# Two feed-forwards to an attention in a fused macaron block: a new order of steps, with residuals kept in DRAM

## The chip, the cores and the metric

The kernel runs on one core of a Trainium2 chip. The metric is the device time of one execution in microseconds (us); lower is better. The core's engines each work through an instruction list of their own, in order, and wait for one another by semaphores: TensorE (PE in the profile), VectorE (DVE), ScalarE (ACT), GpSimd (POOL) and SyncE (SP), which here issues every DMA.

## What is computed

The input is x of 8 batches x 512 tokens x 512 features. Every batch goes through three parts:

```
x = x + 0.5 * ffn(layernorm(x))          # ffn1
x = x + attention(layernorm(x))
x = x + 0.5 * ffn(layernorm(x))          # ffn2

ffn(h):       hidden = silu(h @ W1.T) * (h @ W3.T)         # 2048 wide
              return fwht(hidden) @ W2.T                   # Hadamard transform, normalised
attention(h): q, k, v = rmsnorm(h, qkv_norm_w) @ ternary(qkv_w).T     # 16 heads of 32
              for each of 4 chunks of 128 tokens, with a state S of 32 x 32 a head:
                  o = scale * ((q k^T * decay mask) v + (q * decay) S)
                  S = decay^128 * S + (k * decay)^T v
              return rmsnorm(rmsnorm(o, norm_w), proj_norm_w) @ ternary(proj_w).T
```

All three parts of a batch depend on one another in turn; different batches don't. Both feed-forwards use the same weights.

## The kernel before

Weights are turned, split and (for W2) Hadamard-transformed once, during the first feed-forward, and stay in SBUF. An fp32 value is kept as a sum of two fp16 numbers, high and low; a product of two such values takes three matmuls (high x high, high x low, low x high), and one with the ternary weights two.

**A feed-forward** (`feed_forward`, L211) runs over 16 hidden tiles j of 128. Per tile TensorE does three main steps of 12 matmuls each of 128x512: `gate` j into g_bank, `lin` j into l_bank (L1271), and `down` j - 1 into the four d_banks (L1286). ScalarE takes the silu of g_bank (L742), VectorE multiplies it with l_bank into `hfull` (L986), ScalarE casts the high half (L755), VectorE subtracts for the low half (`low`, L993). g_bank, l_bank, `gate` and `hfull` exist once: gate j + 1 waits for silu j, lin j + 1 for hfull j. At the end VectorE adds the four d_banks to the residual (`resid`, L1001).

**Slots.** The order of all work is written out in one list of steps per place, and every engine walks the same list, doing its part of each step. Between the main steps lie 48 slots: slot 3j stands after gate j, 3j + 1 after lin j, 3j + 2 after low j (down j - 1 stands before low j). Other work is hung into slots.

**The attention** (`attention_slots`, L237) has four head groups g of 128 columns. With b the slot of a group's first scores, b, b + 1, b + 2, b + 3 hold the four `score` steps, b + 2 to b + 5 the four `pv` steps; q(g) is at b - 6 (b - 5 for the first group), k(g) one later, `klow` two later, `kturn` at b - 1; groups are 7 slots apart. q, k and score share bank a_bank0; kturn, kv and pv use a_bank1; v and proj alternate. A score is taken from its bank by VectorE (L1170). q and k are split, stored to DRAM and loaded back into `qs` and `ks` in another layout by SP (L535 to L554). After the last group come `ostat`, the norm `o`, and `proj` (four 8-matmul steps, two banks by turns), whose result VectorE adds to x1 (L1199) to give x2.

**A norm** (`norm_steps`, L227) is three slot entries. `pre`: four bn_stats and seven small operations on VectorE (L1018 to L1038, for `o` L1055 to L1070), a power on GpSimd (L595), `prep` of tile 0. `tr0` and `tr1`: for each tile of 128 tokens VectorE's `prep` into the one buffer `centred` (L1087 and L1090 for qkv, L1092 for o, L1095 else), ScalarE's cast (L764), VectorE's low half `split` (L1111), and a DMA transpose on SP (L560) into an operand buffer: xt for ffn1, zt for q, k, v, yt for o and ffn2. The next tile's prep waits for the split of the one before.

**Places** (PLAN, L419). Batch 0's ffn1 with the preparation of weights (FIRST); batch 1's ffn1 with batch 0's attention; then by turns an ffn2 without attention (SECOND, for batch i - 1, with the norm ffn1 at slots 10, 14, 15 and the norm qkv at 28, 32, 33) and batch i + 1's ffn1 with batch i's attention (WITH_ATTENTION, from slot 0); at the end batch 6's ffn2 with batch 7's attention, and batch 7's ffn2 alone. In the first attention's place and the last one the norm qkv stands at slots 0, 1, 2 and q(0) at 4. The norm ffn2 stands behind proj in the attention's own place (slots 40 to 42, or 44 to 46), and its ffn2 is the next place. x1, x2, qs and ks all lie in SBUF in one tensor `work` and never leave it.

Of the kernel before, what the change touches and what calls it, by code (L numbers as in the profile page):

```python
# [7 lines left out]
ALU = mybir.AluOpType  # L8
ACT = mybir.ActivationFunctionType
AX = mybir.AxisListType  # L10
F32 = mybir.dt.float32
# [3 lines left out]
P = 128  # L15
# [11 lines left out]
def macaron_kernel(nc, x, qkv_w, qkv_norm_w, proj_w, proj_norm_w, norm_w, s, w1, w2, w3, out):  # L27
# [22 lines left out]
    with ctx:  # L50
# [28 lines left out]
        at, start = {}, 0  # L79
        for name, n in sizes.items():  # L80
            at[name] = work[:, start:start + n]
            start += n
# [17 lines left out]
        parts_dram = nc.dram_tensor("parts_dram", [2, 2, P, 2, T], F16, kind="Internal").ap()  # L100

# [82 lines left out]
        q_moved, k_moved = sem("q_moved"), sem("k_moved")  # L184
        k_hi, k_lo, kd_hi, kd_lo = sem("k_hi"), sem("k_lo"), sem("kd_hi"), sem("kd_lo")
# [25 lines left out]
        def feed_forward(which, slots):  # L211
            steps = []
            for j in range(HT):
                steps += [("gate", j)] + slots.get(3 * j, []) + [("lin", j)] + slots.get(3 * j + 1, [])
                if j:
                    steps += [("down", j - 1)]
                steps += [("low", j)] + slots.get(3 * j + 2, [])
            return steps + [("down", HT - 1)] + slots.get(3 * HT, []) + [("resid", (which, t)) for t in range(TT)]
# [18 lines left out]
        def attention_slots(at):  # L237
            slots = {}
            start = at + 5
            for g in range(GROUPS):  # L240
                b = start + (3 + TT) * g
                lead = 6 if g else 5
# [11 lines left out]
            end = start + (3 + TT) * (GROUPS - 1) + 1 + TT  # L254
            pre, tr0, tr1 = norm_steps("o")
            add(slots, end + 1, [("ostat", 0), ("ostat", 1)])
            add(slots, end + 2, [("ostat", 2), ("ostat", 3)])
            add(slots, end + 3, pre)
# [4 lines left out]
            pre, tr0, tr1 = norm_steps("ffn2")  # L263
            add(slots, end + 9, pre)
            add(slots, end + 10, tr0)
            add(slots, end + 11, tr1)
            assert end + 11 <= 3 * HT - 2
            return slots


        def second_slots():
            slots = {}
            for at, which in ((10, "ffn1"), (28, "qkv")):
                pre, tr0, tr1 = norm_steps(which)
                add(slots, at, pre)
                add(slots, at + 4, tr0)
                add(slots, at + 5, tr1)
            return slots

        def late_attention_slots():  # L280
            slots = attention_slots(4)
            pre, tr0, tr1 = norm_steps("qkv")
            return {**slots, 0: pre, 1: tr0, 2: tr1}


# [11 lines left out]
        def first_steps():  # L297
            pre, tr0, tr1 = turned_steps("ffn1")
            steps = [("wsum", 0), ("wscale", 0), pre[0], ("wprep", 0), ("wprep", 1)]
# [44 lines left out]
        WITH_FIRST_ATTENTION = feed_forward("ffn1", late_attention_slots())  # L344
        WITH_ATTENTION = feed_forward("ffn1", attention_slots(0))
        SECOND = feed_forward("ffn2", second_slots())
        SECOND_WITH_ATTENTION = feed_forward("ffn2", late_attention_slots())
        LAST = feed_forward("ffn2", {})

# [16 lines left out]
        def count_uses(steps):  # L366
            fills, copies, uses, before = [0, 0], [0, 0], {}, {}
            for step, arg in steps:
# [11 lines left out]
                for x in (FIRST, WITH_FIRST_ATTENTION, WITH_ATTENTION, SECOND, SECOND_WITH_ATTENTION, LAST)}  # L380

        class Place:
# [4 lines left out]
            def __init__(self, steps, fills, copies, norms, ffn=0, attn=0, block=0, loaded=0, x2=x2, y=yt, x=None):  # L387
                self.steps, self.ffn, self.attn, self.fills, self.copies = steps, ffn, attn, fills, copies
                self.uses, self.before, self.all_fills, self.all_copies = USES[id(steps)]
                self.x2, self.y, self.x, self.block, self.loaded = x2, y, x, block, loaded  # L390
                self.which = "ffn1" if steps in (FIRST, WITH_FIRST_ATTENTION, WITH_ATTENTION) else "ffn2"
                self.source = norms["ffn1" if self.which == "ffn1" else "ffn2"]
                self.norm, self.stats = {}, {}
                for step, arg in steps:
                    if step == "stat":
                        self.norm[arg] = norms["all"]
                        norms["all"] += 1
                        norms["ffn1" if arg == "next" else arg] = self.norm[arg]
# [3 lines left out]
                self.qkv = norms["qkv"]  # L402
# [16 lines left out]
        PLAN = [(FIRST, dict())]  # L419
        for i in range(1, B):  # L420
            PLAN.append((WITH_FIRST_ATTENTION if i == 1 else WITH_ATTENTION, dict(ffn=2 * i - 1, attn=i - 1, block=i, loaded=i)))
            if i < B - 1:
                PLAN.append((SECOND, dict(ffn=2 * i, attn=i, block=i - 1, loaded=i + 1)))
        PLAN += [(SECOND_WITH_ATTENTION, dict(ffn=2 * B - 2, attn=B - 1, block=B - 2, x=(xin, xt))),
                 (LAST, dict(ffn=2 * B - 1, block=B - 1, x2=xin, y=xt))]

        def program(eng, run):
            counts, norms = ([0, 0], [0, 0]), dict.fromkeys(("all", "ln", "ffn1", "qkv", "o", "ffn2"), 0)
            for steps, where in PLAN:
                place = Place(steps, *counts, norms, **where)  # L430
# [4 lines left out]
        def attention_buffers(place):  # L435
            return place.x or (place.x2, place.y)

        def norm_source(place, which):
            return {"ffn1": xin, "next": x_next, "qkv": x1}.get(which) or attention_buffers(place)[0]

        def norm_target(place, which):
            return {"ffn1": xt, "next": xt, "qkv": zt}.get(which) or attention_buffers(place)[1]
# [13 lines left out]
        def _(sp):  # L456
# [55 lines left out]
            def run(place):  # L512
                for step, arg in place.steps:
                    if step == "resid" and arg == ("ffn1", TT - 1):
                        if not (isinstance(place.block, int) and place.block == B - 1):

                            sp.wait_ge(res_done, TT * (place.ffn + 1))
                            sp.dma_start(xin[:], x_tiles[bass.ds((place.block + 1) * TT, TT)].rearrange("t p d -> p t d")
                                         ).then_inc(x_loaded, 16)
                    elif step == "resid" and place.steps is LAST:  # L520
                        t = arg[1]

                        sp.wait_ge(res_done, TT * place.ffn + t + 1)
                        sp.dma_start(out_tiles[place.block * TT + t], xin[:, t, :]).then_inc(y_stored, 16)
                    elif step == "resid" and arg == ("ffn2", TT - 1):

                        sp.wait_ge(res_done, TT * (place.ffn + 1))
                        sp.dma_start(out_tiles[bass.ds(place.block * TT, TT)].rearrange("t p d -> p t d"), x2).then_inc(y_stored, 16)
# [7 lines left out]
                    elif step == "klow":  # L536
# [883 lines left out]
```

## Time and profile before

| | |
|---|---|
| time, median of 3 runs (lowest to highest) | 2546.94 us (2546.01 to 2549.93) |
| the profiled execution's own time | 2551.2 us |
| its span | 2549.5 us |
| mean granted TensorE clock | 0.986 of full |
| busy: TensorE, VectorE, ScalarE, GpSimd | 2392.9, 1185.2, 720.8, 161.6 us (94, 46, 28, 6% of the span) |
| weight loads (beside the matmuls) | 1146.4 us |
| DMA moved | 124.50 MB, mean 49 GB/s |

The profile is of one execution. In the timeline a matmul group's stated duration reaches beyond the start of the next one, since matmuls overlap in the array: 12 matmuls of 128x512 are shown as 2.75 us and start every 2.59 us. Idle time of TensorE is what is in brackets behind a row, with what ended it.

### The profile page before, as it was taken

How to read it: one execution, taken by the hardware profiler on the slowest of the kernel's cores; microseconds unless marked ns; L12 is line 12 of the kernel's file. 1: busy time of each engine (PE TensorE's matmuls, PEld its weight loads, DVE VectorE, ACT ScalarE, POOL GpSimd, SP SyncE). 2: the span in 40 equal slices, each digit the busy share in tenths (PEclk: the TensorE clock that was granted, in tenths of full speed). 3: DMA queues.
4: the chain of work that ended last, by engine and by line, in shares of the span. 5: the costliest groups of instructions: out<-in, count | busy, mean ns of one | idle time of the engine just before them, and what ended most of it. 6: DMA issues, size and time to landing. Idle time of an engine off the chain costs nothing.

```text
span 2549.5 us, 31981 instructions
## 1 busy us (share of the span) xinstructions
PE 2392.9 (94%) x13040; PEld 1146.4 (45%) x13040; DVE 1185.2 (46%) x2087; ACT 720.8 (28%) x1205; POOL 161.6 (6%) x111
## 2 busy tenths in 40 slices
PE   5787999999999999999999999999999999989999
PEld 2243454444544454444544445444444445435444
DVE  6766345334544346334453445443454334644612
ACT  5545332223212232223322232222322223223211
POOL 4710000000000000000000000000000000000000
PEclk9899999999999999999999999999999999999999
DMA  7732112021112111101120110211112011111100
GB/s 214 177 106 60 42 42 50 17 54 42 38 34 34 42 59 27 40 17 58 42 50 17 44 52 26 46 29 42 46 34 50 17 58 42 34 42 59 34 17 17
DMA packets 221393, 124.50 MB, mean 49 GB/s; under 512 B 170176, under 2 KB 194752, under 8 KB 221248
## 3 DMA queue, kind: packets, MB, share of 16 engines
q1 hardware_dynamic: 221248, 122.47, 18.6%
q8 instruction: 103, 1.69, 0.3%
q14 instruction: 42, 0.34, 0.0%
HBM read 56.37 MB, written 25.17 MB: 32 GB/s over the span
## 4 chain that ended last, share of the span: by engine, by line
PE 80%; DVE 10%; issue 4%; DMA 3%; ACT 2%; POOL 1%; SPq 0%; POOLq 0%; DVEq 0%; ACTq 0%
PE l_bank L1271 23%; PE g_bank L1271 22%; PE d_bank L1286 22%; PE a_bank L1327 5%; PE a_bank L1313 2%; PE a_bank L1394 2%; PE a_bank L1381 1%; DVE work L1170 1%; DMA work<-cent 1%; DVE work L986 1%; ACT cent L764 1%; DVE stat L1018 1%; DVE cent L1111 1%; PE a_bank L1375 1%; PE a_bank L1345 1%
## 5 line engine op out<-in xcount | busy, mean ns | idle before, releaser
L1286 PE MATMUL d_bank<-w2t,work 128*128 128x512 f16 x2976 | 687.6, 382 | 9.1 <-DVE work L993 9.1
L986 DVE SCALAR_TENSOR_TENSOR work<-l_bank,l_scale,work 128x512 f32<-128x512 f32 x256 | 191.8, 749 | 673.0 <-PE l_bank L1271 673.0
L1286 PEld LDWEIGHTS d_bank<-w2t,work 128*128 128x128 f16 x2976 | 289.6, 98 | 350.3 <-issue 10.1
L1271 PE MATMUL l_bank<-xt,w3t 128*128 128x512 f16 x1728 | 405.7, 385 | 29.8 <-DVE work L986 29.3
L1271 PE MATMUL g_bank<-xt,w1t 128*128 128x512 f16 x1728 | 398.6, 380 | 16.2 <-ACT work L742 8.9
L742 ACT ACTIVATE work<-g_bank,g_scale 128x512 f32<-128x512 f32 x256 | 175.5, 685 | 533.4 <-PE g_bank L1271 530.9
L755 ACT CAST work<-work 128x512 f16<-128x512 f32 x248 | 153.2, 618 | 602.3 <-DVE work L986 600.7
L1271 PE MATMUL l_bank<-work,w3t 128*128 128x512 f16 x1344 | 308.4, 379 | 0.0
L1271 PE MATMUL g_bank<-work,w1t 128*128 128x512 f16 x1344 | 308.4, 379 | 0.0
L1271 PEld LDWEIGHTS l_bank<-xt,w3t 128*128 128x128 f16 x1728 | 167.6, 99 | 231.5 <-issue 43.4
L1271 PEld LDWEIGHTS g_bank<-xt,w1t 128*128 128x128 f16 x1728 | 166.1, 98 | 214.4 <-ACT work L742 10.5
L993 DVE TENSOR_TENSOR work<-work 128x512 f16<-128x512 f32 x248 | 172.8, 697 | 99.0 <-ACT work L755 98.5
L1271 PEld LDWEIGHTS l_bank<-work,w3t 128*128 128x128 f16 x1344 | 131.2, 98 | 156.9
L1271 PEld LDWEIGHTS g_bank<-work,w1t 128*128 128x128 f16 x1344 | 131.1, 98 | 156.8 <-issue 0.2
L1327 PE MATMUL a_bank<-zt,wqkv 128*128 128x512 f16 x512 | 124.8, 388 | 64.0 <-DVE work L1170 45.8
L764 ACT CAST cent<-cent 128x512 f16<-128x512 f32 x124 | 76.6, 618 | 294.5 <-DVE cent L1095 107.6
L1170 DVE SCALAR_TENSOR_TENSOR work<-a_bank,mask 128x512 f32<-128x512 f32 x128 | 88.0, 687 | 107.1 <-PE a_bank L1345 106.3
L1175 DVE TENSOR_TENSOR work<-work 128x512 f16<-128x512 f32 x128 | 88.6, 692 | 87.5 <-ACT work L825 87.5
L1111 DVE TENSOR_TENSOR cent<-cent 128x512 f16<-128x512 f32 x124 | 85.8, 692 | 79.5 <-ACT cent L764 78.1
L825 ACT CAST work<-work 128x512 f16<-128x512 f32 x128 | 79.0, 617 | 144.1 <-DVE work L1170 143.6
L605 POOL TENSOR_TENSOR work<-qT,lam_t 128x512 f32<-128x512 f32 x32 | 40.7, 1271 | 1092.0 <-PE a_bank L1381 744.9
L1327 PEld LDWEIGHTS a_bank<-zt,wqkv 128*128 128x128 f16 x512 | 46.6, 99 | 123.7 <-DVE work L1170 54.0
(194 smaller groups left out, 1580.9 us busy)
## 6 DMA issues: line engine op xcount, KB each, us to landing
work<-parts_dram SPq DMA_DIRECT2D x192, 128.0 KB, 2.6
w2t<-in_L_ffn_W_dram SPq DMA_DIRECT2D x32, 256.0 KB, 3.3
xin<-in_L_attn_x_dram SPq DMA_DIRECT2D x8, 1024.0 KB, 5.1
parts_dram<-q_parts SPq DMA_DIRECT2D x32, 256.0 KB, 2.0
parts_dram<-k_parts SPq DMA_DIRECT2D x32, 256.0 KB, 2.1
out_dram<-work SPq DMA_DIRECT2D x7, 1024.0 KB, 4.3
work<-in_L_ffn_W_dram SPq DMA_DIRECT2D x8, 512.0 KB, 5.1
w2t<-in_L_attn_qkv_w_dram SPq DMA_DIRECT2D x6, 512.0 KB, 4.9
```

What stands on the lines that cost most here:

```text
L742: nc.scalar.activation(gate, g_bank[:], ACT.Silu, scale=g_scale[:, j:j + 1]).then_inc(gate_ready, 1)
L755: nc.scalar.copy(hidden(place, j)[:, 0, :], hfull).then_inc(hi_ready, 1)
L764: nc.scalar.copy(halves[:, t % 2, 0, :], centred).then_inc(ln_hi, 1)
L825: nc.scalar.copy(sc[:, c % 2, 0], flow.rearrange("p (h t) -> p h t", h=HG)).then_inc(sc_hi, 1)
L986: nc.vector.scalar_tensor_tensor(out=hfull, in0=l_bank[:], scalar=l_scale[:, j:j + 1], in1=gate, op0=ALU.mult, op1=ALU.mult).then_inc(hful ...
L993: nc.vector.tensor_tensor(parts[:, 1, :], hfull, parts[:, 0, :], ALU.subtract).then_inc(lo_ready, 1)
L1111: nc.vector.tensor_tensor(halves[:, t % 2, 1, :], centred, halves[:, t % 2, 0, :], ALU.subtract).then_inc(ln_lo, 1)
L1170: nc.vector.scalar_tensor_tensor(out=masked, in0=a_bank[b][:].rearrange("p (h t) -> p h t", h=HG), scalar=SCORE_SCALE, in1=mask[:, HG * g: ...
L1175: nc.vector.tensor_tensor(sc[:, c % 2, 1], masked, sc[:, c % 2, 0], ALU.subtract).then_inc(sc_lo, 1)
L1271: ins = nc.tensor.matmul(dst[:], wt[:, wp, k, P * j:P * (j + 1)], src[:, xp, k, :], start=(k == 0 and wp == xp), stop=(k == KT - 1 and wp ...
L1286: ins = nc.tensor.matmul(d_bank[t][:], parts[:, hp, P * t:P * (t + 1)], w2t[:, wp, j, :], start=(j == 0 and hp == wp), stop=(j == HT - 1 a ...
L1327: ins = nc.tensor.matmul(a_bank[b][:], wqkv[:, k, col:col + P], src[:, part, k, :], start=(k == 0 and part == 0), stop=(k == KT - 1 and pa ...
```

## The change

- A place may now hold two feed-forwards (96 slots). `begin` marks where each starts. Batches 1 to 6 each have such a place (MIDDLE, LAST_MIDDLE): ffn1 of batch i + 1, then ffn2 of batch i - 1, with the attention of batch i over both. So batch i's ffn2 comes one ffn later than before.
- In it the groups are 14 slots apart and q leads the scores by 6; in the first and last attention they are 8 apart, with a lead of 4. With b = 18, 32, 46, 60 the four pv steps end at slot 65, the norm o stands at 69 to 71, proj at 73 and 74. First attention: b = 8, 16, 24, 32, norm o at 41 to 43, proj at 45 and 46. Last: b = 4, 12, 20, 28, norm o at 37 to 39, proj at 41 and 42, norm ffn2 at 43 to 45.
- Norms in a two-feed-forward place: ffn2 (batch i - 1) at 0, 2, 4, qkv (batch i) at 6, 8, 10, q(0) at 12, ffn1 of the next place at 78, 80, 82; in the last such place ffn2x (76, 78, 80) and qkv7 (82, 84, 86) instead. The first attention's place has the extra norm `third` at 13, 15, 17.
- Operand buffers: xt holds the operand of ffn2, yt that of ffn1, zt that of q, k, v and of proj.
- x1 is stored to DRAM at the end of each ffn1 and fetched into x2 behind the norm o (`fetch`); proj's result is added there. x2 is stored behind proj (`keep`) and comes back (`back`, two slots ahead of the last proj) into `res`, the space of qs and ks, where ffn2's result is added and stored to the output.

In the waits at its end, `sp`, `act` and `dve` are SP's, ScalarE's and VectorE's lists: `klow` on SP, `v` on ScalarE, `proj` on VectorE.

```diff
-        def feed_forward(which, slots):
-            steps = []
+        def feed_forward(i, which, slots, base=0):
+            steps = [("begin", i)]
...
-        def attention_slots(at):
-            slots = {}
-            start = at + 5
+        def attention_slots(slots, b, period, lead):
             for g in range(GROUPS):
-                b = start + (3 + TT) * g
-                lead = 6 if g else 5
                 add(slots, b - lead, [("q", g)])
                 add(slots, b - lead + 1, [("qlow", g), ("k", g)])
                 add(slots, b - lead + 2, [("klow", g)])
...
+                end = b + 2 + TT
+                b += period
...
             add(slots, end + 4, tr0)
-            add(slots, end + 5, tr1)
+            add(slots, end + 5, tr1 + [("fetch", 0)])
             add(slots, end + 7, [("proj", 0), ("proj", 1)])
-            add(slots, end + 8, [("proj", 2), ("proj", 3)])
...
+            add(slots, end + 8, [("proj", 2), ("proj", 3), ("keep", 0)])
+            return end + 8
+
+        def norm_slots(slots, at, which, gap=2):
+            steps = norm_steps(which)
+            for i in range(3):
+                add(slots, at + gap * i, steps[i])
+
+        def first_slots():
+            slots = {}
+            norm_slots(slots, 0, "qkv", 1)
+            add(slots, 3, [("early", 0)])
+            attention_slots(slots, 8, 8, 4)
+            norm_slots(slots, 13, "third")
             return slots
...
+        def middle_slots(last):
             slots = {}
...
+            norm_slots(slots, 0, "ffn2")
+            norm_slots(slots, 6, "qkv")
+            at = attention_slots(slots, 18, 14, 6)
+            add(slots, at - 2, [("back", 0)])
+            if last:
+                norm_slots(slots, at + 2, "ffn2x")
+                norm_slots(slots, at + 8, "qkv7")
+            else:
+                norm_slots(slots, at + 4, "ffn1")
             return slots
...
+        def last_slots():
+            slots = {}
+            at = attention_slots(slots, 4, 8, 4)
+            add(slots, at - 2, [("back", 0)])
+            norm_slots(slots, at + 1, "ffn2", 1)
...
+        MIDDLE = feed_forward(0, "ffn1", middle_slots(False)) + feed_forward(1, "ffn2", middle_slots(False), 3 * HT)
...
+                        sp.wait_ge(res_done, TT * (f.n + 1))
...
+                        sp.dma_start(x1_dram[f.batch % 2], x1).then_inc(x1_stored, 16)
...
+                    elif step == "fetch":
+
+                        sp.wait_ge(ln_norm, TT * (place.norm["o"] + 1))
+                        sp.wait_ge(x1_stored, 16 * (place.attn + 1))
+                        sp.dma_start(x2, x1_dram[place.attn % 2]).then_inc(x1_back, 16)
+                    elif step == "keep":
...
+                        sp.dma_start(x2_dram[place.attn % 2], x2).then_inc(x2_stored, 16)
+                    elif step == "back":
...
+                        sp.wait_ge(x2_stored, 16 * (batch + 1))
+                        sp.dma_start(res, x2_dram[batch % 2]).then_inc(x2_back, 16)
...
+                        elif place.attn >= 2:
+
+                            sp.wait_ge(y_stored, 16 * (place.attn - 1))
...
+                        if t == 0 and place.attn:
+
+                            act.wait_ge(x2_stored, 16 * place.attn)
+                            act.wait_ge(ln_norm, TT * (place.ffn2 + 1))
...
+                        dve.wait_ge(x1_back, 16 * (a + 1))
+                        nc.vector.scalar_tensor_tensor(out=x2[:, t, :], in0=a_bank[b][:],
+                                                       scalar=proj_scale[:], in1=x2[:, t, :], op0=ALU.mult,
```

## Rows read from the trace of the kernel before

**Rows 1.** Busy time by stretch: from:to length, busy (x instructions) per engine, TensorE clock, DMA.

```profile
410.00:548.00 138.00, 133.50 (x609) 59.90 (x608) 52.90 (x98) 28.39 (x45) 3.02 (x3) 0.98 0.16 31
848.00:1008.00 160.00, 153.58 (x969) 77.81 (x967) 79.13 (x138) 47.62 (x77) 6.09 (x5) 1.00 0.16 47
1008.00:1148.00 140.00, 138.80 (x643) 62.65 (x642) 53.75 (x100) 29.70 (x47) 3.02 (x3) 1.00 0.14 31
```

**Rows 2.** Waits of TensorE over the whole span: total us, times, longest.

```profile
PE a_bank L1327 <- DVE work L1170: 45.8, 48, 1.2
...
PE g_bank L1271 <- ACT work L742: 8.9, 9, 1.9
...
PE a_bank L1313 <- ACT kT L799: 4.1, 6, 0.7
...
PE a_bank L1327 <- DMA zt<-cent: 18.2, 2, 9.1
...
PE d_bank L1286 <- DVE work L993: 9.1, 2, 4.6
```

**Rows 3.** Timeline, TensorE: start, duration, engine, line; idle before and releaser.

```profile
43.13 2.76 PE L1271 MATMUL g_bank<-xt,w1t 128*128 128x512 f16 x12 [2.92 <-DMA w1t<-cent]
...
423.32 4.99 PE L1286 MATMUL d_bank<-w2t,work 128*128 128x512 f16 x12 [4.50 <-DVE work L993]
...
2249.37 3.57 PE L1327 MATMUL a_bank<-zt,wqkv 128*128 128x512 f16 x8 [9.08 <-DMA zt<-cent]
```

**Rows 4.** Timeline, a place's start and the qkv norm at slots 0 to 2.

```profile
2229.78 2.75 PE L1271 MATMUL g_bank<-work,w1t 128*128 128x512 f16 x12
...
2230.80 2.47 DVE L1018 BATCH_NORM_STATS2 stat<-work 128x6 f32<-128x512 f32 x4
...
2245.48 0.69 DVE L1111 TENSOR_TENSOR cent<-cent 128x512 f16<-128x512 f32 x1 [0.68 <-ACT cent L764]
```

**Rows 5.** Timeline, the ffn2 norm's first and last step; a gate in one.

```profile
409.77 2.46 DVE L1018 BATCH_NORM_STATS2 stat<-work 128x6 f32<-128x512 f32 x4
...
421.97 0.69 DVE L1111 TENSOR_TENSOR cent<-cent 128x512 f16<-128x512 f32 x1 [0.68 <-ACT cent L764]
...
1017.95 2.76 PE L1271 MATMUL g_bank<-xt,w1t 128*128 128x512 f16 x12 [1.14 <-ACT work L742]
```

**Rows 6.** Timeline, the o norm and proj in a steady place.

```profile
977.79 0.69 DVE L1045 BATCH_NORM_STATS2 stat<-work 128x6 f32<-128x512 f32 x1
...
989.71 0.69 DVE L1111 TENSOR_TENSOR cent<-cent 128x512 f16<-128x512 f32 x1
...
994.20 3.62 PE L1394 MATMUL a_bank<-wproj,work 128*128 128x512 f16 x16
...
996.44 0.69 DVE L1111 TENSOR_TENSOR cent<-cent 128x512 f16<-128x512 f32 x1 [0.69 <-ACT cent L764]
...
1000.24 3.63 PE L1394 MATMUL a_bank<-wproj,work 128*128 128x512 f16 x16
```

**Rows 7.** DMA by kind with us to landing; issue time of transposes, ns.

```profile
zt<-cent SPq DMA_TRANSPOSE x32, 3.0
...
xin<-in_L_attn_x_dram SPq DMA_DIRECT2D x8, 1024.0 KB, 5.1
...
out_dram<-work SPq DMA_DIRECT2D x7, 1024.0 KB, 4.3
...
L560 SPq DMA_TRANSPOSE zt<-cent x32: 1231/1232/2121, 244.3 to 2246.2; - x32
```

**Rows 8.** Timeline, k of a first head group; landing of parts.

```profile
859.95 1.89 PE L1327 MATMUL a_bank<-zt,wqkv 128*128 128x512 f16 x8
...
863.88 0.34 SPq L543 DMA_DIRECT2D parts_dram<-k_parts  x1
...
865.96 1.25 SPq L554 DMA_DIRECT2D work<-parts_dram  x3
...
work<-parts_dram SPq DMA_DIRECT2D x192, 128.0 KB, 2.6
```

More of the change, by code:

```diff
@@ L205, in macaron_kernel @@
         decay_top, decay_fit = sem("decay_top"), sem("decay_fit")
-        def feed_forward(which, slots):
-            steps = []
+        def feed_forward(i, which, slots, base=0):
+            steps = [("begin", i)]
             for j in range(HT):
-                steps += [("gate", j)] + slots.get(3 * j, []) + [("lin", j)] + slots.get(3 * j + 1, [])
+                steps += [("gate", j)] + slots.get(base + 3 * j, []) + [("lin", j)] + slots.get(base + 3 * j + 1, [])
                 if j:
                     steps += [("down", j - 1)]
-                steps += [("low", j)] + slots.get(3 * j + 2, [])
-            return steps + [("down", HT - 1)] + slots.get(3 * HT, []) + [("resid", (which, t)) for t in range(TT)]
+                steps += [("low", j)] + slots.get(base + 3 * j + 2, [])
+            return steps + [("down", HT - 1)] + [("resid", (which, t)) for t in range(TT)]
         def turned_steps(which):
@@ L397, in __init__ @@
                         norms["all"] += 1
-                        norms["ffn1" if arg == "next" else arg] = self.norm[arg]
+                        norms[{"next": "ffn1", "third": "ffn1", "ffn2x": "ffn2", "qkv7": "qkv"}.get(arg, arg)] = self.norm[arg]
                         if arg != "o":
@@ L416, in known_zero, with norm_source, norm_target @@
             return isinstance(v, int) and v <= 0
[L419 to L425, printed above, removed]
-        def program(eng, run):
-            counts, norms = ([0, 0], [0, 0]), dict.fromkeys(("all", "ln", "ffn1", "qkv", "o", "ffn2"), 0)
-            for steps, where in PLAN:
-                place = Place(steps, *counts, norms, **where)
+        PLAN = [(FIRST, 0, (("ffn1", 0, xt),)), (WITH_FIRST_ATTENTION, 0, (("ffn1", 1, xt),))]
+        for i in range(1, B - 1):
+            PLAN.append((MIDDLE if i < B - 2 else LAST_MIDDLE, i, (("ffn1", i + 1, yt), ("ffn2", i - 1, xt))))
+        PLAN += [(WITH_LAST_ATTENTION, B - 1, (("ffn2", B - 2, yt),)), (LAST, B - 1, (("ffn2", B - 1, xt),))]
+        def program(eng, run):
+            counts, n = ([0, 0], [0, 0]), 0
+            norms = dict.fromkeys(("all", "ln", "ffn1", "qkv", "o", "ffn2"), 0)
+            for steps, attn, ffns in PLAN:
+                ffns = [FeedForward(n + i, *f) for i, f in enumerate(ffns)]
+                n += len(ffns)
+                place = Place(steps, *counts, norms, ffns, attn)
                 run(place)
                 counts = place.after()
[L435 to L442, printed above, removed]
+        def norm_source(which):
+            return {"ffn1": xin, "next": x_next, "third": x1, "qkv": x1, "qkv7": x1}.get(which, x2)
+        def norm_target(steps, which):
+            return {"ffn2": xt, "ffn2x": yt, "third": yt, "qkv": zt, "qkv7": zt, "o": zt}.get(which, xt if steps is FIRST else yt)
         def flips(m, t):
@@ L513, in run @@
                 for step, arg in place.steps:
[L514 to L518, printed above, removed]
+                    if step == "begin":
+                        f = place.ffns[arg]
+                    elif step == "resid" and arg == ("ffn1", TT - 1):
+                        sp.wait_ge(res_done, TT * (f.n + 1))
+                        if f.batch >= 2:
+                            sp.wait_ge(x1_back, 16 * (f.batch - 1))
+                        sp.dma_start(x1_dram[f.batch % 2], x1).then_inc(x1_stored, 16)
+                        if f.batch < B - 1:
+                            sp.dma_start(xin[:], x_tiles[bass.ds((f.batch + 1) * TT, TT)].rearrange("t p d -> p t d")
                                          ).then_inc(x_loaded, 16)
@@ L768, in run @@
                         act.wait_ge(a_ready[b], fill)
-                        nc.scalar.copy(norm_target(place, which)[:, 0, :, P * t:P * (t + 1)],
+                        nc.scalar.copy(norm_target(place.steps, which)[:, 0, :, P * t:P * (t + 1)],
                                        a_bank[b][:].rearrange("p (k t) -> p k t", k=KT)).then_inc(a_free[b], 1)
@@ L1251, in run @@
                         j = arg
-                        src = xt if place.which == "ffn1" else place.y
+                        src = f.x
                         wt, dst, done = (w1t, g_bank, g_ready) if step == "gate" else (w3t, l_bank, l_ready)
```

149 lines of the change are left out of this document (82 added, 67 removed).

## The prediction

> **What bounds the kernel now.** I read four views in this order. First the busy time by stretch [rows 1]: from about 250 us the program repeats every 300 us, a feed-forward with a batch's attention (848 to 1008) and one without (1008 to 1148). TensorE is busy for 153.58 of 160 us and 138.80 of 140 us, at full granted clock. It is the bound, and in a steady pair it idles for 6.4 + 1.2 = 7.6 us. The change leaves TensorE's matmuls as they are, so only waits can be won or lost. Second, the waits by releaser [rows 2] name these: the q and k matmuls wait for the copy of the masked scores out of the bank they share, 45.8 us in 48 waits, six in each of 8 batches (5.7 us a batch). In each of the 6 steady pairs (batches 1 to 6) a gate matmul also waits 1.1 us for ScalarE's silu, and the value matmul 0.7 us for ScalarE's copy of k (4.1 in 6). At the ends two q matmuls wait 9.1 us for the turned operand of a norm, and two `down` matmuls wait 4.5 to 4.6 us because VectorE's low half of the last hidden tile stands behind a norm. Third, a long wait has a second price [rows 3]: behind 4.50 us of idle, 12 matmuls took 4.99 us instead of 2.75, the 1.2 GHz level instead of 2.4, and the stretch's mean granted clock is 0.98; behind 9.08 us, 8 took 3.57 instead of 1.89 and the next 12 0.6 more. So 2.2 to 2.3 us. Behind 2.92 us there was no such loss. Fourth, the timeline gives the chains that the change moves [rows 4 to 8].
>
> **What is removed.** (a) In the two-feed-forward places q(g+1) comes at slot b+8 with the last score at b+3; in the first and last attention at b+4. Both stand apart from the scores by a main step (12 matmuls, 2.59 us from start to start), longer than the 0.69 us copy: -45.8. (b) The silu wait behind the old ffn2 norm and the k copy's wait, 1.8 us in 6 pairs: -10.8, and the last attention's silu wait -1.1. (c) The last attention begins with its operand ready, since the norm `qkv7` ran at slots 82 to 86 of the place before: -9.1 and -2.3 of slow matmuls. (d) The first attention is no longer followed by the ffn2 norm: -4.5 - 2.2. The other 9.1 us wait (first place, norm at slots 0 to 2, q at slot 4) stays as it is. Sum: 45.8 + 10.8 + 1.1 + 11.4 + 6.7 = **75.8 us removed**.
>
> **What is added, first: two norms ahead of q(0), six times.** Norms ffn2 (slots 0, 2, 4) and qkv (6, 8, 10) now precede q(0) at slot 12. From the start of the place TensorE has 12 main steps ahead of q(0): 12 x 2.59 = 31.1 us. VectorE has one serial chain, since all tiles pass through one `centred`. It begins 1.0 us after TensorE starts, behind the residual adds [rows 4]. A qkv norm lasts from 2230.80 to 2245.48 + 0.69 = 2246.17, 15.4 us, in which stand 1.5 us of feed-forward work: 13.9. The ffn2 norm lasts from 409.77 to 422.66, less 0.75 of feed-forward work: 12.1 [rows 5]. Between them VectorE must also do hfull and low of tiles 0 to 2 and hfull of tile 3, 4 x 0.75 + 3 x 0.69 = 5.1. Then the last transpose lands 3.0 us after its issue (3.1 with the hand-over) [rows 7]. 1.0 + 12.1 + 13.9 + 5.1 + 3.1 = 35.2, against 31.1: at least 4.1 us late. On top, ScalarE's order is written out: its casts for slots 2 and 8 stand ahead of silu(1) and silu(3), which free g_bank and feed VectorE; that is the 1.14 us wait of a gate matmul inside the old norm [rows 5]. Following the three engines step by step I get 0.4 us lost at gate 2, 0.2 at lin 3, 2.1 at gate 4 and 4.6 at q(0), 7.2 in all. I take 6.5, bounds 4.1 and 7.5. The wait at q(0) is of the size behind which matmuls were slow: +2.2 (0 to 2.2). Before, the norm of q had 15 slots' lead in the feed-forward without attention, and this cost nothing.
>
> **Second: x1 returns from DRAM, eight times.** The residual add of `proj` 0 now waits on x1_back. The fetch is issued on SP's queue behind the last transpose of the o norm. In the trace VectorE ends that norm's last tile at 996.44 + 0.69 = 997.13 [rows 6]; SP spends 1.23 us on issuing the transpose, and a transfer of 1024 KB lands 5.1 us after its issue [rows 7]: 997.2 + 1.2 + 5.1 = 1003.5. TensorE can start proj 2 at 1000.24 only because the add of proj 0, which empties its bank, was done; now that add ends at 1003.5 + 0.75 = 1004.3, 4.0 us too late. That is the last place's phase. In the two-feed-forward places the o norm starts 0.9 us behind the end of a lin matmul instead of 0.9 us ahead of a gate matmul, 1.8 us later against TensorE, with the same six main steps to proj 0 and one main step between proj 1 and proj 2. Its first transpose lands 1.1 us late for proj 0 (0.8 us to spare in the trace: 989.71 + 0.69 + 3.0 = 993.4 against 994.20), the second 0.5; the waits for the fetch are then 4.3. Queued behind it on VectorE is low of tile 8, which isn't due for two main steps. I take 1.6 + 4.3 = 5.9 for each of the six; 4.3 + 0.3 in the first attention (o norm at slots 41 to 43), 4.0 in the last. Slow matmuls may or may not follow a 4.0 to 4.3 us wait (4.50 did it, 2.92 didn't): half of 2.2. Lower bound for a fetch: rows of 8 KB instead of 2 KB and no slow matmuls, 3.5; upper: the 1024 KB of `back`, issued 0.4 us behind it on the same queue, share the 16 engines and add up to 2.6 (half of 5.1), and 2.2.
>
> The Trainium skill, "DMA: Bandwidth & Descriptors", section "Anatomy of one DMA", gives some 2.0 us fixed plus bytes at 436 GB/s, an estimate of 4.4 us for this transfer; the row says 5.1, and by the page each fetch would cost 0.7 us less, 6 us over the run. Its "Rules for kernel authors" say to issue a DMA early and to wait on it late; the change issues this one two slots ahead of its use, with x2 free only then, and by that rule this is where it loses.
>
> **Third, small.** The first and last attention have q four slots ahead of the scores, k three. From the end of a k matmul three main steps and a kturn pass, 8.1 us. In the trace [rows 8] k's matmuls end at 861.8, its store issues at 863.88, the loads start 2.1 us later, and with three issues of 0.43 us and 2.6 us to land they are there at 869.5, 7.7 us behind; where `klow` stands behind a lin tile's hfull 2.1 us more. I take 3.0 for the three later groups in each of the two places (0 to 6), and 0.7 in each for v(0) right behind k (the same wait as before). The last ffn2 norm stands one slot earlier but behind an hfull: its `down` wait grows from 4.6 to 5.5, +0.9. The last two-feed-forward place puts two norms (76 to 86) close behind proj: +2.0. The other new transfers (x1 store with x's load at the end of an ffn1, x2 store, `back`) have 10 slots or more to land; SP's next entries are 6 slots off, so I cost them at nothing; were that cover gone, a wait would be one transfer, 5.1 us. The one queue entry that stands close is klow(0) of the last attention behind y_stored: y is issued 1.1 us into that place and lands 4.3 us later [rows 7], k's parts come at about 11 us.
>
> **Sum.** Six places: 6 x (6.5 + 2.2 + 5.9 + 1.1) = 94.2. First attention: 3.0 + 0.7 + 0.3 + 4.3 + 1.1 = 9.4. Last: 3.0 + 0.7 + 4.0 + 1.1 = 8.8. Rest: 2.9. **115.3 us added**, 75.8 removed: +39.5. On the profiled execution's own 2551.2 us (span 2549.5) that is 2590.7; it stands 4.3 us above the median 2546.94, which becomes **2586 us**.
>
> **The rivals.**
> (1) Forecast, waits as above, 0.58. Its own range: no slow matmuls at all and the lower bounds of the norm chain, 39.5 - 6 x (2.4 + 2.2 + 1.1) - 2.2 = +3, to the upper ones, about +65; most of it +20 to +60.
> (2) The fetch is hidden: if the transfer lands by the time that the add of proj 0 would run anyway (3 to 4 us sooner than the rows say), 6 x 5.4 + 5.4 + 5.1 = 42.9 us go: 2543, no change or slightly faster. Against it: no row of the steady part shows 1024 KB landing in under 4.3 us [rows 7]. Chance 0.12.
> (3) Faster, by one mechanism: VectorE runs the two norms ahead of TensorE so that q(0) finds its operand, and the fetch is hidden too. It decides at 31.1 us of chain from the place's start; then the six places cost 1.6 each, 9.6 + 4.0 + 3.7 + 2.9 = 20.2 against 75.8: 2491. If only q(0) is free and the fetch bites, 39.5 - 6 x 8.7 = -12.7: 2534. For it: idle of VectorE is 54% of the span. Against it: the chain is serial, with rows for each link, and 35.2 > 31.1. Chance 0.17.
> (4) Crowded transfers: fetch and `back` share the engines, 2.6 us more in six places and slow matmuls behind every wait (1.1 in each of eight): 39.5 + 15.6 + 8.8 = +64: 2611. The trace shows two 1024 KB transfers side by side nowhere in its steady part. Chance 0.13.
>
> **How the numbers follow.** The likeliest is 2586. Leaving one in ten on either side takes in half of (3) below and most of (4) above: 2522 to 2614. About 0.2% (5 us) is what a measurement of this kernel can tell. Faster by more: 0.17 of (3) and a third of (2), 0.20. Within: most of the rest of (2) and the lower edge of (1), 0.08. Slower: 0.72.
>
> **What would show it.** In the profile after: the waits of q and k matmuls for the score copy (45.8 us) gone but for a rest; a new wait of the first q matmul for the zt transposes, 4 to 5 us, six times; a gate matmul waiting some 2 us for silu just ahead of it; the add of proj 0 waiting for a DMA into `work` from x1_dram, and proj 2 behind it for 4 us, eight times; 12 matmuls of 4.9 us behind these waits and a granted clock under 1.00 in every place. If instead the first q matmul starts without a wait, or the add of proj 0 starts at once, rivals (3) or (2) hold. The prediction is wrong if the two chains of VectorE overlap in a way that the rows of single norms don't show.

## The result, and the profile after

The changed kernel takes 2593.49 us in the median of 4 runs (2592.87 to 2593.69) against 2546.76 before: 1.0181 times as long, with a 95% interval of 1.0163 to 1.0198. It is slower by some 47 us; 2586 had been forecast. The page of its profile:

```profile
span 2591.1 us, 32092 instructions
...
PE 2419.5 (93%) x13040; PEld 1151.8 (44%) x13040; DVE 1189.9 (46%) x2087; ACT 722.1 (28%) x1205; POOL 161.4 (6%) x111
...
work<-x_dram SPq DMA_DIRECT2D x16, 1024.0 KB, 5.8
```

The span grew by 41.6 us (2591.1 against 2549.5). TensorE runs the same 13040 matmuls, yet is "busy" for 26.6 us more (2419.5 against 2392.9), and its idle time grew by the other 15.0 us. In the first 250 us, where both kernels run the same 800 matmuls, it is busy for 183.9 us against 180.6 and idle for 3.3 us less (in five of the versions below it was busy for 180.9 to 183.5 there). Behind those 250 us, busy time grew by 23.3 us, which goes with matmuls at half clock, and idle time by 18.3. The mean granted clock fell from 0.986 to 0.973 of full.

The waits of TensorE by releaser (total, times, longest), to be read beside [rows 2]:

```profile
PE a_bank L1460 <- DVE work L1263: 36.9, 8, 5.5
...
PE a_bank L1393 <- DMA zt<-cent: 33.2, 7, 9.1
...
PE g_bank L1337 <- ACT work L796: 12.5, 8, 2.0
...
PE a_bank L1460 <- DMA zt<-cent: 8.8, 14, 1.1
...
PE a_bank L1411 <- DMA work<-parts_dram: 7.3, 3, 4.2
...
PE d_bank L1352 <- DVE work L1051: 5.5, 1, 5.5
```

The 45.8 us in 48 waits of q and k matmuls for the score copy have gone altogether. New at the top is L1460, the `proj` matmul: eight waits, one a batch, for the VectorE add at L1263. L1393 holds q: of its 33.2 us, 9.1 are the first attention's, which stood before too, and 24.1 are new, one wait in each of the six two-feed-forward places. Two stretches of a steady place, read as [rows 1] (TensorE's granted clock is the third number from the end):

```profile
1032.00:1180.00 148.00, 141.43 (x772) 67.43 (x771) 63.45 (x114) 38.65 (x62) 4.54 (x4) 0.98 0.16 40
1180.00:1340.00 160.00, 153.66 (x830) 73.02 (x828) 70.15 (x122) 38.30 (x61) 4.54 (x4) 0.98 0.21 63
```

At 1.00 in [rows 1]'s steady pair, the granted clock is 0.98 in both halves now. From one place's q(0) to the next one's it is 1084.28 - 776.87 = 307.4 us, where the pair of places before took 300:

```profile
776.87 3.22 PE L1393 MATMUL a_bank<-zt,wqkv 128*128 128x512 f16 x8 [4.58 <-DMA zt<-cent]
```

**Where the two long waits come from.** The timeline from the start of that place to q(0) (start, duration, engine, line; idle before and its releaser in brackets):

```profile
1046.28 2.75 PE L1337 MATMUL g_bank<-work,w1t 128*128 128x512 f16 x12
1047.18 2.46 DVE L1081 BATCH_NORM_STATS2 stat<-work 128x6 f32<-128x512 f32 x4
...
1063.14 2.47 DVE L1081 BATCH_NORM_STATS2 stat<-work 128x6 f32<-128x512 f32 x4
...
1076.20 0.68 ACT L796 ACTIVATE work<-g_bank,g_scale 128x512 f32<-128x512 f32 x1
...
1076.93 2.76 PE L1337 MATMUL g_bank<-work,w1t 128*128 128x512 f16 x12 [1.99 <-ACT work L796]
...
1080.37 0.69 DVE L1174 TENSOR_TENSOR cent<-cent 128x512 f16<-128x512 f32 x1 [0.68 <-ACT cent L818]
...
1084.28 3.57 PE L1393 MATMUL a_bank<-zt,wqkv 128*128 128x512 f16 x8 [4.58 <-DMA zt<-cent]
...
1087.64 4.03 PE L1337 MATMUL l_bank<-work,w3t 128*128 128x512 f16 x12
```

TensorE starts the place at 1046.28, VectorE the first norm at 1047.18 and the second at 1063.14. Its last split ends at 1080.37 + 0.69 = 1081.06, the transpose lands and q starts at 1084.28, 38.0 us into the place, 4.58 us idle. Ahead of it silu(3) starts only at 1076.20 behind ScalarE's casts, and gate 4 waits 1.99 us for it. The 8 matmuls of q then take 3.57 us instead of 1.89, and the 12 of the lin behind them 4.03 instead of 2.75.

Then the stretch around proj in the place before:

```profile
972.62 1.89 PE L1460 MATMUL a_bank<-wproj,zt 128*128 128x512 f16 x8 [1.04 <-DMA zt<-cent]
...
975.45 0.69 DVE L1174 TENSOR_TENSOR cent<-cent 128x512 f16<-128x512 f32 x1 [0.68 <-ACT cent L818]
...
977.50 0.53 SPq L559 DMA_DIRECT2D work<-x_dram  x1
978.13 0.37 SPq L578 DMA_DIRECT2D work<-x_dram  x1
983.34 1.41 DVE L1263 SCALAR_TENSOR_TENSOR work<-a_bank,proj_scale,work 128x512 f32<-128x512 f32 x2 [6.50 <-DMA work<-x_dram]
...
984.15 5.31 PE L1460 MATMUL a_bank<-wproj,zt 128*128 128x512 f16 x16 [4.82 <-DVE work L1263]
```

The last split of the o norm ends at 976.14; SP issues its transpose, and at 977.50 the fetch of x1 (L559), at 978.13 the load of x2 (L578). VectorE sits idle for 6.50 us until the fetch has landed, adds at 983.34, and proj 2 starts at 984.15 after 4.82 us of idle. Its 16 matmuls with proj 3 take 5.31 us instead of 3.62 [rows 6]. All eight batches show this wait, 4.13 to 5.49 us long.

### The profile page after: what moved, and what is told of

Its sections match the earlier page's. It is cut to its first block, busy times and chain, and to the rows that moved or that the text cites. A ratio compares the mean times of both kernels' runs of the same rounds, so it can differ in the third digit from the quotient of the medians.

```text
span 2591.1 us, 32092 instructions
## 1 busy us (share of the span) xinstructions
PE 2419.5 (93%) x13040; PEld 1151.8 (44%) x13040; DVE 1189.9 (46%) x2087; ACT 722.1 (28%) x1205; POOL 161.4 (6%) x111
## 4 chain that ended last, share of the span: by engine, by line
PE 72%; DVE 14%; DMA 5%; issue 4%; ACT 3%; POOL 1%; SPq 1%; DVEq 0%; POOLq 0%; ACTq 0%
PE l_bank L1337 20%; PE d_bank L1352 20%; PE g_bank L1337 19%; PE a_bank L1393 5%; PE a_bank L1379 2%; DVE cent L1174 2%; DMA zt<-cent 2%; PE a_bank L1460 2%; DMA work<-x_dram 1%; DVE work L1044 1%; PE a_bank L1447 1%; DVE stat L1081 1%; ACT cent L818 1%; PE a_bank L1411 1%; DMA xt<-cent 1%
## 5 line engine op out<-in xcount | busy, mean ns | idle before, releaser
L1393 PE MATMUL a_bank<-zt,wqkv 128*128 128x512 f16 x512 | 131.8, 404 | 33.2 <-DMA zt<-cent 33.2
L1460 PE MATMUL a_bank<-wproj,zt 128*128 128x512 f16 x256 | 75.5, 455 | 45.7 <-DVE work L1263 36.9
```

What stands on the lines that cost most here:

```text
L1393: ins = nc.tensor.matmul(a_bank[b][:], wqkv[:, k, col:col + P], src[:, part, k, :], start=(k == 0 and part == 0), stop=(k == KT - 1 and pa ...
L1460: ins = nc.tensor.matmul(a_bank[b][:], src[:, part, k, P * t:P * (t + 1)], wproj[:, k, :], start=(k == 0 and part == 0), stop=(k == KT - 1 ...
```

## The experiments

Times are given as ratios to the kernel before, timed beside them on the same chip (2548.60 us in the first four, 2549.48 in the others); 0.001 is 2.5 us. The changed kernel stands at 1.0181.

**1. x1 fetched by tiles.** As soon as a tile of x2 has been read by the o norm its space is free, so the fetch needn't wait for all four.

```diff
-            add(slots, end + 5, tr1 + [("fetch", 0)])
+            add(slots, end + 5, tr1)
...
                                                halves[:, t % 2].rearrange("p a d -> p (a d)")).then_inc(flipped[t % 2], 16)
+                        if which == "o":
+                            sp.wait_ge(x1_stored, 16 * (place.attn + 1))
+                            sp.dma_start(x2[:, t, :], x1_dram[place.attn % 2, :, t, :]).then_inc(x1_back[t], 16)
...
-                        dve.wait_ge(x1_back, 16 * (a + 1))
+                        dve.wait_ge(x1_back[t], 16 * (a + 1))
```

> The changed kernel, but x1 is fetched in four tiles of 256 KB, each on SP's queue behind the transpose of the same tile of the o norm, with a semaphore for each tile. Theory (the add of proj 0 waits for x1, and proj 2 for the add): the eight waits of proj 2, 36.9 us in the changed kernel's profile, go, and with them the slow proj matmuls behind them (proj is busy for 75.5 us against 58.5 before): -54 us, 2540. Rival A (the transposes suffer: each stands behind 0.4 us of issue and shares the engines with 256 KB): the waits of proj 0 and 1 for turned tiles, now 8.8 us, grow by 0.5 us a tile, some 8 us in all: 2548. Rival B (something else, as the down steps or VectorE's order, would hold TensorE there anyway): 2580 or more, with another wait named at proj 2.

Measured: 2546.78 us (median of 10), ratio 0.9993 (0.9983 to 1.0002), 48 us less than the changed kernel. TensorE's waits:

```profile
PE a_bank L1393 <- DMA zt<-cent: 34.9, 7, 9.1
...
PE a_bank L1460 <- DMA zt<-cent: 14.5, 14, 1.5
PE g_bank L1337 <- ACT work L796: 13.2, 9, 2.0
```

The 36.9 us of proj 2 for the add are gone and proj is busy for 59.1 us instead of 75.5. The waits of proj 0 and 1 for turned tiles grew from 8.8 to 14.5 us, as rival A had it (8 expected, 5.7 found). So the theory holds with rival A's correction: this one transfer cost 48 us, as much as the net loss of 47.

**2. The attention two slots later.**

```diff
-            at = attention_slots(slots, 18, 14, 6)
+            at = attention_slots(slots, 20, 14, 6)
```

> The changed kernel, but in the six two-feed-forward places the whole attention stands two slots later (b = 20, 34, 48, 62; q(0) at slot 14), the two norms ahead of it unchanged. Theory (the chain of two norms ends 4 to 5 us behind the slot of q(0)): two slots are 5.2 us of main steps, so the waits of the first q matmul, 33.2 - 9.1 = 24.1 us, go, and some 13 us of slow matmuls behind them (q, k matmuls busy 131.8 against 124.8, and about 1.3 us of the lin behind in each); the 2.0 us wait of a gate matmul for silu stays: -37 us, 2556. Rival (VectorE is short of time there, so its delay shows at whatever comes next): the wait turns up at lin, v or the scores, and the time stays within 5 us of 2593.

Measured: 2555.72 us (median of 10), ratio 1.0029 (1.0020 to 1.0039), 39 us less.

```profile
PE a_bank L1460 <- DVE work L1263: 37.6, 8, 5.7
...
PE g_bank L1337 <- ACT work L796: 13.5, 9, 2.0
...
PE a_bank L1393 <- DMA zt<-cent: 9.1, 1, 9.1
```

Only the first attention's 9.1 us are left of q's waits; the gate's waits for silu stay, and the slow matmuls behind q are gone (122.6 us for these matmuls against 131.8). Little took their place: six waits of `pv` for VectorE to take `kv` from the bank (L1244), 3.5 us in all. So VectorE is late at q(0), and hardly elsewhere. Not all of the 39 us belongs to q: the edit moves the whole attention, the o norm and proj with it, and the waits of proj 0 and 1 for turned tiles fell from 8.8 us to 1.7. Gate 4 still waits 1.99 us in the six places, and the 12 matmuls behind took 4.4 us instead of 2.76 in four of them, where it was two in the changed kernel.

**3. Both.**

```diff
-            at = attention_slots(slots, 18, 14, 6)
+            at = attention_slots(slots, 20, 14, 6)
...
+                        if which == "o":
+                            sp.wait_ge(x1_stored, 16 * (place.attn + 1))
+                            sp.dma_start(x2[:, t, :], x1_dram[place.attn % 2, :, t, :]).then_inc(x1_back[t], 16)
```

> Both edits together: x1 fetched by tiles, the attention two slots later. Theory (two separate waits): -54 - 37 = -91 us, 2502, which would be 45 us under the kernel before. Rival (the two share a cause, as the slow clock that one leaves to the other): less than the sum, 2515 to 2530.

Measured: 2512.34 us, ratio 0.9858 (0.9843 to 0.9872). Against the changed kernel 0.0323, where the two edits alone give 0.0188 + 0.0152 = 0.0340: they add up but for 4 us, no more than the intervals leave open. The two waits are separate. The forecast of 2502 was 10 us too low. One thing it didn't have: behind gate 4's wait the matmuls were now slow in all six places, some 1.7 us each (the timeline row below is one of them).

```profile
PE g_bank L1337 <- ACT work L796: 12.5, 7, 2.0
PE a_bank L1393 <- DMA zt<-cent: 9.1, 1, 9.1
...
PE a_bank L1460 <- DMA zt<-cent: 7.3, 8, 1.3
```

```profile
1046.19 4.45 PE L1337 MATMUL g_bank<-work,w1t 128*128 128x512 f16 x12 [1.99 <-ACT work L796]
```

**4. What the spread of the head groups wins.** The version of experiment 2, with the groups 7 slots apart again.

```diff
-            at = attention_slots(slots, 20, 14, 6)
+            at = attention_slots(slots, 44, 7, 6)
```

> As the version with the attention later, but with the head groups 7 slots apart as in the kernel before, in the middle of the place (b = 44, 51, 58, 65; q(0) at slot 38), so that q(g+1) and k(g+1) again stand right behind scores. Compared with the version with b = 20. Theory (the spread alone wins what the score waits cost): six waits a place, 5.7 us, come back in six places: +34 us, 2590. Rival A (the spread wins nothing, since TensorE's lost time returns elsewhere): within 5 us of the version with b = 20. Rival B (the stores of x1 and the load of x at slot 48 collide with the parts of q and k): +34 and up to 4 us more a place, as a wait of scores for a DMA.

Measured: 2601.09 us, ratio 1.0207 (1.0192 to 1.0222): 0.0178, or 45 us, above experiment 2.

```profile
PE a_bank L1393 <- DVE work L1233: 34.4, 36, 1.2
...
PE a_bank L1401 <- ACT work L885: 9.4, 6, 1.6
```

The score waits are back, 36 of them in six places, 34.4 us as expected. Most of the other 10 us has a source that no theory named: in six places a `kturn` waits, 9.4 us in all, for L885, ScalarE's copy of a group's result out of a_bank1. It is a matter of where the groups lie, not of their density: b = 44 puts the last `pv` of the first group at slot 49 and the `kturn` of the second at 50, behind the first tile of a feed-forward, which has no `down` step between them, and ScalarE's copy (585.98 + 0.68) is not done when TensorE comes:

```profile
584.69 0.46 PE L1447 MATMUL a_bank<-work 128*128 128x32 f16 x12
...
585.98 0.68 ACT L885 ACTIVATE work<-a_bank,o_scale 128x512 f32<-128x512 f32 x1
...
586.72 0.55 PE L1401 MATMUL a_bank<-ident,kT 128*128 128x128 f32 x3 [1.57 <-ACT work L885]
```

Rival B's wait of scores for a DMA didn't come: waits for parts were 8.0 us in three against 7.2. So the saving that the change was credited with is real; it was more than offset.

**5. Do the fetch and the load of x2 crowd each other?**

```diff
-            add(slots, at - 2, [("back", 0)])
+            add(slots, at + 1, [("back", 0)])
```

> The changed kernel, but in the six two-feed-forward places the load of x2 for the second feed-forward is issued three slots later, behind proj, so that it doesn't share the DMA engines with the fetch of x1. Theory (they are served in turn, sharing costs little): the fetch's landing moves from 5.4 us (5.1 to 5.8) to 5.1 to 5.3, the eight waits of proj 2 from 36.9 us to some 35, time within 5 us of 2593. Rival (crowded transfers): the landing falls by 1 us or more, the waits to under 30 us, time 2585 or less.

Measured once: 2587.17 us, 6.3 us less than the changed kernel (8 by the ratios to the kernel before) and so outside the theory's 5 us. Proj 2's waits are 33.9 us instead of 36.9. The fetch's issue time in ns and its landing, first of the changed kernel, then of this one:

```profile
L559 SPq DMA_DIRECT2D work<-x_dram x8: 512/523/525, 413.0 to 2429.7; - x8
...
DMA to landing us min/median/max: 5.1/5.4/5.8
```

```profile
L559 SPq DMA_DIRECT2D work<-x_dram x8: 514/523/527, 411.3 to 2421.8; - x8
...
DMA to landing us min/median/max: 4.9/5.0/5.2
```

Sharing costs 0.4 us in the median. One transfer of 1024 KB alone is what makes the add wait: the landing and proj 2's waits are near the theory's numbers and far from the rival's. Of the time, 3.0 us are proj 2's. The waits of q fell as well, from 33.2 us to 28.2, but that is no gain: behind gate 4's wait the matmuls were slow in five of the six places instead of two, so TensorE came to q(0) later. What the rest of the gain of this single run comes from stays open.

**6. The extra norm of the first attention.** The changed kernel has a 4.15 us wait of scores for the parts of k:

```profile
300.01 2.46 DVE L1081 BATCH_NORM_STATS2 stat<-work 128x6 f32<-128x512 f32 x4
...
305.52 0.68 DVE L1196 TENSOR_TENSOR k_parts<-kT,k_parts 128x512 f16<-128x512 f32 x1
...
306.23 0.34 SPq L593 DMA_DIRECT2D parts_dram<-k_parts  x1
...
312.17 0.59 PE L1411 MATMUL a_bank<-work 96*128 96x128 f16 x4 [4.15 <-DMA work<-parts_dram]
```

The statistics of the norm `third` start at 300.01; the low half of k (L1196) comes only at 305.52 on the same list, its store at 306.23.

```diff
-            norm_slots(slots, 13, "third")
+            norm_slots(slots, 14, "third")
```

> The changed kernel, but in the first attention's place the norm of batch 2's x stands at slots 14, 16, 18 instead of 13, 15, 17, and so behind the low half of k of the second head group on VectorE's list instead of ahead of it. Theory (the 4.15 us wait of scores for the k parts at 312 us in the changed kernel comes from that norm's statistics standing ahead of k's low half): this wait falls under 1 us, others stay, -4 to -6 us. Rival (the wait comes from the short lead of 4 slots and the transfers): it stays at 4 us.

Measured once: 2592.06 us, 1.4 us less (3.6 by the ratios); for a single run neither is clear of the spread, 2545.86 to 2551.30 for the kernel before. The waits for parts fell from 7.3 us in three to 3.1 in two, so the norm was the cause of the long one. But two others came near it, 3.0 us:

```profile
316.02 0.47 PE L1447 MATMUL a_bank<-work 128*128 128x32 f16 x12 [1.98 <-DVE work L1244]
...
324.51 1.90 PE L1393 MATMUL a_bank<-zt,wqkv 128*128 128x512 f16 x8 [1.05 <-DVE work L1233]
```

So most of the wait moved with the norm. That suggests, from this one run, that VectorE has too much work at this spot of a dense attention, whichever step it delays.

**7. The qkv norm one slot later**, on top of experiment 3.

```diff
-            norm_slots(slots, 6, "qkv")
+            norm_slots(slots, 7, "qkv")
```

> Fetch by tiles and attention two slots later, and in addition the qkv norm of the six places at slots 7, 9, 11 instead of 6, 8, 10, so that ScalarE's casts of tiles 1 and 2 stand behind silu(3) instead of ahead of it. Theory (ScalarE's written order makes gate 4 wait 2.0 us for silu 3): the six waits, 12 us, go and no other comes: 2500. Rival (VectorE's chain is what is late, ScalarE only the messenger): the wait moves to a lin, or to the first q matmul, and the time stays within 3 us of 2512.

Measured: 2510.81 us, ratio 0.9855 (0.9840 to 0.9870), no different from experiment 3. The six waits of gate 4 for silu are gone (1.1 us is left of 12.5), and q waits again, in six places, 14.5 us in all:

```profile
1035.95 0.75 DVE L1044 SCALAR_TENSOR_TENSOR work<-l_bank,l_scale,work 128x512 f32<-128x512 f32 x1 [1.38 <-PE l_bank L1337]
...
1052.56 0.69 DVE L1174 TENSOR_TENSOR cent<-cent 128x512 f16<-128x512 f32 x1 [0.69 <-ACT cent L818]
...
1056.45 3.40 PE L1393 MATMUL a_bank<-zt,wqkv 128*128 128x512 f16 x8 [2.40 <-DMA zt<-cent]
```

The rival was right. With this slot VectorE's hfull(2) stands ahead of the norm's statistics and waits 1.38 us for its lin (first row), and its low(3) stands ahead of the split of tile 2. The statistics start 19.0 us into the place instead of 16.9 in experiment 3, and the last split (second row) ends 35.6 us into it instead of 34.8, while TensorE, which lost nothing at gate 4, comes to q(0) sooner. Of interest is the third row: only 2.40 us of idle, and the 8 matmuls take 3.40 us instead of 1.89. It was so in five of the six places (3.40 to 3.53); in the first of them they took 1.89 us behind 2.41 us of idle.

**8. A version with room in all of these places.**

```diff
-            add(slots, end + 7, [("proj", 0), ("proj", 1)])
-            add(slots, end + 8, [("proj", 2), ("proj", 3), ("keep", 0)])
-            return end + 8
+            add(slots, end + 7 + late, [("proj", 0), ("proj", 1)])
+            add(slots, end + 8 + late, [("proj", 2), ("proj", 3), ("keep", 0)])
+            return end + 8 + late
...
-            norm_slots(slots, 13, "third")
+            norm_slots(slots, 14, "third")
...
-            norm_slots(slots, 6, "qkv")
-            at = attention_slots(slots, 18, 14, 6)
+            norm_slots(slots, 8, "qkv")
+            at = attention_slots(slots, 24, 13, 6, 1)
```

`late` is 1 in the six places and 0 in the other two; the fetch is by tiles.

> A version meant to beat both: fetch of x1 by tiles; in the six places the qkv norm at 8, 10, 12 and q(0) at 18 (b = 24, groups 13 apart), proj one slot later behind the o norm; the third norm at slots 14, 16, 18. Theory: against the version with both edits (2512) the gate's waits for silu (some 10 us), proj's for turned tiles (7.3 us) and 4 us of the k parts' go: 2490. Rival (each slot is as good as the next; the waits move): 2505 to 2515.

Measured: 2486.72 us, ratio 0.9758 (0.9741 to 0.9774), 2.4% under the kernel before and 4.1% under the changed one. What each of the moves gave isn't separated; together they stand 0.0100 (25 us) under experiment 3.

```profile
span 2483.4 us, 32114 instructions
...
PE 2380.3 (96%) x13040; PEld 1145.4 (46%) x13040; DVE 1190.2 (48%) x2087; ACT 721.1 (29%) x1205; POOL 161.5 (7%) x111
```

```profile
PE d_bank L1352 <- DVE work L1051: 15.8, 8, 5.7
...
PE a_bank L1393 <- DMA zt<-cent: 9.1, 1, 9.1
```

TensorE is busy 12.6 us less than in the kernel before, with the same matmuls. In part that is because fewer of them follow a long wait (the granted clock is 0.988 against 0.986). In part it may be the profile's way of counting: 12 matmuls are shown 0.16 us longer than they take (2.75 against 2.59), and this shows as busy ahead of each wait; for the 48 score waits that are gone it makes an estimated 7.7 us. What is left behind the first feed-forward is in the main the 9.1 us of the first attention and waits of `down` for VectorE's low half, 15.8 us in eight; they have grown by 10 (1.6 us in each of the six places, and 0.6), and a better place for the norms at the end of the six places may yet win some of them. That wasn't tried.

## Why the prediction was right

The time came out 7.5 us above the forecast, within its range, and the mechanisms are those of its first rival. Step by step, in us:

| step | forecast | measured |
|---|---|---|
| (a) score waits removed | 45.8 | 45.8, no such wait left |
| (b) waits for silu and for the copy of k removed | 11.9 | 11.7 (7.6 and 4.1), none left at these places |
| (c), (d) end effects: last q(0) ready, first `down` free | 13.6 of waits | both gone |
| two norms: gate 4 | 2.1 by steps | 1.99 |
| two norms: q(0) | 4.6 by steps | 4.57 or 4.58 in four places, 2.88 in two |
| gate 2 and lin 3 | 0.6 a place | 0.21 and 0.34, once each |
| proj 0 and 1, turned tiles | 1.6 a place | 1.4 a place |
| fetch of x1, six places; first; last | 4.3; 4.3; 4.0 | 4.21 to 5.49; 4.39; 4.13 |
| waits for parts of k, both ends | 6.0 | 7.3 |
| `down` wait ahead of the last feed-forward | 5.5 | 5.51 |
| slow matmuls, added less removed | 17.5 | busy time grew by 23.3 behind the first 250 us (26.6 in all) |

**Right, and shown.** The chain of the two norms comes, with the 7.2 us worked out step by step, to 31.1 + 7.2 = 38.3 us from the place's start to the landing (the four parts named add up to 7.3; the bound by plain sums, 35.2, left out the waits between the engines). It was 38.0, and experiment 2 shows that two slots end the wait of q(0), though not gate 4's. The fetch was put at 5.1 us to land and a 4.3 us wait; it landed in 5.4, and experiment 1 shows 48 us for it and its slow matmuls, net of 6 us of longer waits for the transposes. Experiment 4 confirms the credit side.

**Mis-sized.** The term that was too small is that of slow matmuls, and in it the half of 2.2 us given to each fetch, 8.8 us in all, reasoning that a 4.50 us wait had slowed matmuls and one of 2.92 had not [rows 3]. In fact proj was busy for 75.5 us instead of 58.5, 17.0 us in eight waits, 1.4 to 2.8 each and never none. The 2.2 us for each q(0) were about right: with the lin behind it 1.3 to 3.0, 11.7 in six against 13.2; the 1.7 + 1.3 = 3.0 of the timeline above is the largest. Gate 4's wait was given no slow matmuls, and in two of the six places cost 1.7 us of them. The idle time, on the other side, was forecast too high: 39.5 less the 17.5 for slow matmuls is 22, and it was 15.0, or 18.3 behind the first 250 us. So the total's closeness is partly luck of two opposite misses.

**Missed.** The norm `third` was costed at nothing without naming what stands behind it on VectorE's list; there it was the low half of k, and the wait was 4.15 us (experiment 6). The forecast had 3.0 us for such waits in that place, for another reason (the short lead), so the sum hid the omission. The 2.0 us given to the two norms close behind proj in the last two-feed-forward place didn't show.

**The rivals.** That the fetch is hidden (2) and that q(0) finds its operand (3) are refuted by the waits named. Crowded transfers (4) exist, but the fetch lost 0.4 us by them instead of 2.6; the slow matmuls behind every fetch, which this rival also had, did come.

By the Trainium skill ("DMA: Bandwidth & Descriptors", "Anatomy of one DMA") the fetch would land after an estimated 4.4 us. The page gives its fit for transfers issued by GpSimd, and this one is SP's; the trace has 5.1 to 5.8, and 4.9 to 5.2 with nothing behind it. Its advice in "Rules for kernel authors", to issue early and wait late, is what experiment 1 does: the same bytes, each quarter issued when its space comes free.

## What to carry to other kernels

When a schedule is loosened at one place, list for every moved or added step what then stands behind it on its engine and what transfer it waits for; here 46 us of small waits were won and 8 transfers that came 4 to 5 us late, with 6 norms packed ahead of their user, took all of it and 47 us more. A buffer that comes free piece by piece can be refilled piece by piece (48 us here). And a wait of TensorE is to be priced at its length plus what the matmuls behind it lose.

## What was not expected of the hardware

- Slow matmuls began behind shorter waits than thought, and not always. Behind 2.40 us of idle, 8 matmuls took 3.40 us instead of 1.89 (experiment 7), while behind 2.92 us in [rows 3] 12 matmuls took the usual 2.76, and at one place of experiment 7 the 8 matmuls took 1.89 behind 2.41 us. In the changed kernel itself gate 4 waits 1.99 us in each of the six places, with the same steps ahead of it; in four the 12 matmuls behind took 2.76 us, as at 1076.93 above, in two 4.45:

```profile
1386.93 4.45 PE L1337 MATMUL g_bank<-work,w1t 128*128 128x512 f16 x12 [1.99 <-ACT work L796]
1394.26 3.43 PE L1393 MATMUL a_bank<-zt,wqkv 128*128 128x512 f16 x8 [2.88 <-DMA zt<-cent]
```

  In these two, TensorE came to q(0) later and so waited 2.88 us instead of 4.58 for it. Gate 4's wait of 1.99 us was followed by slow matmuls in four of six places in experiment 2, and in all six in experiment 3. The length of the wait alone doesn't decide whether the clock falls; what does stays open.
- Two transfers of 1024 KB issued 0.6 us apart on one queue cost the first little: it landed in 5.4 us in the median instead of 5.0. The second took 7.2 us in the median, but also 6.9 when it was issued later (experiment 5), so what slowed it isn't shown.
- 256 KB pieces issued between the transposes made TensorE's waits for these 5.7 us longer, in 14 waits (experiment 1).
